# Normalising: ten constant products on TensorE beside VectorE's statistics

## What is computed

```python
def _layernorm(x, axis=-1, eps=1e-05):
    m = jnp.mean(x, axis=axis, keepdims=True)
    v = jnp.var(x, axis=axis, keepdims=True)
    return (x - m) / jnp.sqrt(v + eps)

x = x + _L0_xattn_ref(_layernorm(x, axis=-1), fside_BxSxS_0, ctx_1024, ctx_1024, ...)
x = x + _L0_attn_ref(_layernorm(x, axis=-1), L0_attn_q_w, ...)
x = x + _L0_ffn_ref(_layernorm(x, axis=-1), L0_ffn_w1s, ...)
x = x + _L1_xattn_ref(_layernorm(x, axis=-1), ctx_1024, ctx_1024, ...)
...
x = x + _L3_ffn_ref(_layernorm(x, axis=-1), L3_ffn_Wq, ...)
```

## Time and profile before

| | |
|---|---|
| median of 3 runs | 2808.99 us (2806.58 to 2811.42) |
| profiled execution | 2812.88 us, span 2811.0 us |
| TensorE busy in the span | 2357.8 us (84%) |
| VectorE busy | 1502.4 us (53%) |
| ScalarE busy | 1047.6 us (37%) |
| GpSimd busy | 300.6 us (11%) |
| mean granted TensorE clock | 0.88 |

### The profile page before, as it was taken

The page is one execution under the profiler, slowest core; times in us unless marked ns, Lnnn a source line. Parts: engine busy times, 40 slices in busy tenths (PEclk is TensorE's granted clock), DMA queues, the critical chain, the costliest instruction groups (busy, mean ns, idle before and its releaser), DMA issues. The chain is left out here.

```text
span 2811.0 us, 38689 instructions
## 1 busy us (share of the span) xinstructions
PE 2357.8 (84%) x15016; PEld 1377.6 (49%) x15016; DVE 1502.4 (53%) x2414; ACT 1047.6 (37%) x1874; POOL 300.6 (11%) x595
## 2 busy tenths in 40 slices
PE   2999999778998798999995866866879799698778
PEld 1344444335797463444443542432227657365447
DVE  4778777332221457888863862337986433223433
ACT  2566666412110234777772641213212233021310
POOL 2453000000000300000001510100000000000100
PEclk8899999987999897999997677876778899888889
DMA  6977443010453897555420001001004440200200
GB/s 188 244 184 168 92 91 61 26 69 1 180 225 129 258 279 187 95 121 98 92 30 33 12 1 58 28 1 61 0 0 150 154 161 1 92 3 0 99 0 8
DMA packets 108214, 258.60 MB, mean 92 GB/s; under 512 B 11808, under 2 KB 83072, under 8 KB 94080
## 3 DMA queue, kind: packets, MB, share of 16 engines
q1 hardware_dynamic: 101696, 203.71, 27.5%
q0 software_dynamic: 2736, 39.37, 4.1%
q10 hardware_dynamic: 3600, 13.04, 1.2%
HBM read 211.26 MB, written 44.83 MB: 91 GB/s over the span
## 5 line engine op out<-in xcount | busy, mean ns | idle before, releaser
L666 DVE TENSOR_REDUCE sta_parts<-sta_psA 128x1 f32<-128x1024 f32 x544 | 625.8, 1187 | 188.3 <-PE sta_psA L583 186.6
L724 ACT ACTIVATE sta_probs<-sta_psS 128x512 f32<-128x512 f32 x1056 | 575.9, 597 | 274.8 <-PE sta_psS L594 272.8
L594 PE MATMUL sta_psS<-L_xattn_qS,L_xattn_kst 99*128 99x256 bf16 x2112 | 356.3, 278 | 11.4 <-ACT sta_probs L724 6.6
L583 PE MATMUL sta_psA<-L_xattn_kst,L_xattn_qS 99*128 99x512 bf16 x1088 | 293.3, 387 | 46.9 <-PEq L59 32.1
L594 PEld LDWEIGHTS sta_psS<-L_xattn_qS,L_xattn_kst 99*128 99x128 bf16 x2112 | 161.4, 98 | 259.4 <-ACT sta_probs L724 183.1
L603 PE MATMUL sta_psO<-sta_probs,L_xattna_V 128*32 128x256 f32 x2560 | 189.5, 385 | 0.0
L583 PEld LDWEIGHTS sta_psA<-L_xattn_kst,L_xattn_qS 99*128 99x128 bf16 x1088 | 104.3, 99 | 131.7 <-DVE sta_parts L666 43.8
L202 ACT ACT_TABLE_LOAD x14 | 18.0, 1283 | 339.0 <-PEq L59 339.0
L2357 PE MATMUL l2t_psY<-l2t_hc,top_consts_weights 128*128 128x512 f32 x128 | 93.5, 845 | 30.7 <-DVE l2t_hc L2393 30.6
L603 PE MATMUL sta_psO<-sta_probs,L_xattn_V 128*32 128x256 f32 x1536 | 114.8, 390 | 0.0
L1008 ACT ACTIVATE sht_probs<-sht_psS 128x768 f32<-128x768 f32 (+1 forms) x64 | 55.3, 863 | 152.8 <-PE sht_psS L852 101.3
(11 more groups left out here) (617 smaller groups left out, 3973.5 us busy)
## 6 DMA issues: line engine op xcount, KB each, us to landing
L_xattn_kst<-L_xattn_keys SPq DMA_DIRECT2D x186, 136.0 KB, 5.0
L_xattn_kst<-L_xattn_keys SPq DMA_DIRECT2D x186, 128.0 KB, 4.6
L_xattn_values<-prj_rows SPq DMA_DIRECT2D x64, 256.0 KB, 3.7
L_xattn_keys<-prj_parts SPq DMA_DIRECT2D x32, 384.0 KB, 4.0
L_xattna_V<-in_ctxV SPq DMA_DIRECT2D x5, 2048.0 KB, 11.8
L_xattna_V<-L_xattn_values SPq DMA_DIRECT2D x5, 2048.0 KB, 11.0
l2f_W<-in_M SPq DMA_DIRECT2D x10, 1024.0 KB, 7.6
L_xattn_keys<-sta_bparts SPq DMA_DIRECT2D x24, 384.0 KB, 8.2
```

What stands on the lines that cost most here:

```text
L583: last = nc.tensor.matmul(psA[:, u % 2, col:col + rhs.shape[1]], lhsT, rhs, start=True, stop=True)
L594: last = nc.tensor.matmul(psS[:, at % 2, j * T:(j + 1) * T], lhsT, rhs, start=True, stop=True)
L666: nc.vector.tensor_reduce(into(parts[:, u // n % 2]), view(psA[:, u % 2, :]), AX.X, ALU.max).then_inc(max_taken, 1)
L724: nc.scalar.activation(probs[:, u % NP, i * 512:(i + 1) * 512], psS[:, at % 2, :], ACT.Exp, scale=scale).then_inc(probs_ready, 1)
```

## The change

TensorE gets ten matrix products at the start of the stage, ahead of its wait for the first tile. Each multiplies `ident16` by `mask16` and writes one PSUM bank, `psI`, that nobody reads. No semaphore is tied to them. This happens in 13 of the 15 calls: not in that of L0_xattn, where `ident16` and `mask16` aren't there yet, and not in the last, which returns before it. Nothing is removed.

```diff
-def normalize(nc, K, X, xn, xnT, eps, rms=False, w=None):
+def normalize(nc, K, X, xn, xnT, eps, rms=False, w=None, fill=True):
...
         psT = p.ps("psT", [P, KC, 512])
+        psI = p.ps("psI", [P, 512])
...
             @block.tensor
             def _(pe):
                 if xnT is None:
                     return
+                for _ in range(10 if fill else 0):
+                    nc.tensor.matmul(psI[:], K["ident16"], K["mask16_q"], start=True, stop=True)
                 for t in range(NT):
                     pe.wait_ge(rows_ready, t + 1)
...
-                normalize(nc, K, X, xn, xnT, 1e-5)
+                normalize(nc, K, X, xn, xnT, 1e-5, fill=False)
```

## The result

| | before | after |
|---|---|---|
| median | 2808.34 us (2806.45 to 2811.42, 6 runs) | 2797.82 us (2793.30 to 2799.62, 6 runs) |
| profiled execution, span | 2812.88 us, 2811.0 us | 2799.62 us, 2797.8 us |
| mean granted clock | 0.88 | 0.892 |

The ratio is 0.9962, with a 95% interval from 0.9951 to 0.9973: 10.5 us or 0.4% faster. The spans of the two traces differ by 13.2 us, more than the medians do: the traced execution of before was 4.5 us above its median, that of the changed kernel 1.8 us.

What follows compares the result with a forecast made beforehand. TensorE, often at the low clock, was taken as the bound behind the calls. Gains of 17.5, 1.5 and 0.9 us less 3.0 and 1.0 gave 15.9 us; 2797.0 less 3.9 for the median gave 2793 us, range 2784 to 2806.

Steps and rivals of the forecast that it cites:

- What bounds the kernel: Whole kernel: TensorE is busy 84% of the time, and behind the calls it is the bound at the low clock.
- The cost of the ten products: At the stage's start: ten cost 4.3 us at the low clock, 2.2 us at the high; room 2.98 us.
- The delays in the low calls: Six plain calls whose stage starts at low clock: later transposes lose 0.5 us each, 3.0 us in all.
- the five high calls: Calls whose stage starts at high clock: faster transposes gain 0.3 us in each of five, 1.5 us in all.
- The products behind: Behind eight plain calls: high clock halves 34.95 us of products, 17.5 us gained, 1.0 us taken off for misses.
- one third of a stretch: L0_attn, behind a wait of 3.08 us: one third of half of 5.66 us counted, 0.9 us gained.
- the sum: Whole kernel: 17.5 + 1.5 + 0.9 - 3.0 - 1.0 = 15.9 us gained, forecast 2793 us.
- rival D: Whole kernel: fill dropped or too late, or gains given back in later stages; time stays 2809 us; chance 0.05.
- A: At the fills: the clock takes no notice of this work, which only delays, 10 us; 2819 us; chance 0.1.
- B: Between fill and products: clock rises but falls again, half of eight stretches missed, 7.7 us gained, 2801 us; chance 0.15.
- C: Clock also holds in L0_attn and two root-mean-square calls, delays small: 24 us gained, 2785 us; chance 0.1.

## Why the prediction was right, and where it wasn't

**What bounds the kernel: right.** Behind the calls TensorE was the bound, and its clock alone was missing: with the same number of products but one row, which leaves the clock low, nothing is won and 14 us are lost.

**The cost of the ten products: right.** They ran at 0.43 us apiece at the low clock and 0.22 at the high one. Where the stage starts high nothing was delayed.

**The delays in the low calls: half as large.** Forecast 3.0 us. The transposes end 4.93 (L0_attn), 5.27 (L1_xattn), 6.06 (L1_attn), 5.49 (L2_xattn), 4.82 (L3_xattn) and 4.62 us (L3_attn) after the start; against 4.95 that is 1.5 us in sum. The extra 0.6 to 0.8 us in three of these calls with fourteen products didn't show in the total. In the five high calls for which 1.5 us of gain were forecast the transposes end 2.3 us sooner in sum.

**The products behind: right near the calls.** With delays and transposes 15.9 us were forecast, and 15.5 are there at the ends of the stretches of this trace. L2_ffn missed its stretch, L1_attn had nearly the full delay; L2_xattn and L3_ffn came as worked out. L0_attn, for which one third of a stretch was counted, has none of it here and far more in other traces.

**The step that failed is the sum.** It added up the stretches and let each gain reach the end of the program. It gave 10 us to the calls that start high and 6.6 us to the low ones. Measured apart, the high ones bring 0.0006 of the time, 1.7 us, with at most 6.7 us; that error is clear. The low ones bring 11.5 us (6.5 to 16.6), which is more by its middle, though 6.6 us is just inside. If the middles hold, the two errors have opposite signs, and it is in part luck that the total of 10.5 us came out inside the range. Of the 5.4 us between the forecast gain and the measured one, 0.4 are missing at the stretches' ends and 2.3 in the sections; the other 2.7 are the difference between the pair of traces and the medians. The prediction named the mechanism as its rival D, "given back in later stages", but only for all of the gain and with 0.05. It belonged into the sum, as a share of every term.

**The rivals.** A falls: the clock rises on zeros too, when all rows are at work. Had the clock taken no notice, its price of 10 us would have been too low, as the one-row kernel shows. B, a clock that falls before the products, occurred in L2_ffn and L0_attn of the changed kernel's trace; it isn't what took most of the missing time. Its 2801 us is 3 us from the median, nearer than the forecast of 2793, but not for its reason. C's clock that holds in L0_attn came in three traces without anything done for it.

**What stays open.** The lengths of sections over all the traces repeat a part of the pattern. With a fill of full rows in the call, L1_xattn takes 580.6 to 583.3 us (eight traces) and 584.3 to 585.2 without one (five), L2_xattn 135.0 to 139.6 against 138.1 to 142.4; by their middles both win more than was forecast. L0_ffn, among kernels with one row in the clearing of psY, takes 238.5 to 238.9 against 239.3 to 239.9: about half is kept. L3_ffn keeps 0.3 of 2.6 us. L2_attn takes some 247 us in five of its seven traces with a fill, longer than the 245.6 of the kernel before, but also in three of six without one. Why the low calls raise what they win while the high ones lose it isn't shown beyond the two places seen (L0_ffn's rise, L3_ffn's fall) and a section that answers to a shift of 0.93 us with 2.8. And since the unchanged kernel differs by 3.8 us in one section from one trace to the next, the share of luck in the 11.5 us isn't known.

## What to carry to other kernels

Where TensorE waits while another engine works and then bounds the next stage at the low clock, fill the wait with products that use all 128 rows (fewer columns weren't tried); zeros will do. Between seven and fourteen products no difference could be told in the total, though seven left the clock low in two calls. Look for work that keeps TensorE busy without raising its clock, such as clearing a bank with one row, and try it with all its rows: the clock rose sooner, but that it shortens the whole isn't shown. A few us won before a long, uneven stretch may not be there at its end: measure such calls apart, over several executions, and don't add up windows of one trace.

## What the runs showed of the hardware

- With ten products of one row of 128 and the transposes behind them TensorE was busy for 6.17 of 6.20 us, and the clock stayed at 0.50 (ratio 1.0050); 128 rows of zeros raised it (0.9958) just as data did (0.9962).
- The same wait of 3.08 us in L0_attn, behind the same ten products, left the clock high in one trace (four products in 1.95 us behind it) and low in another (3.75 us).
- The section of L3_ffn became 2.8 us longer for a delay of 0.93 us and 3.4 us longer for one of 1.85 us, and no shorter for 2.6 us won inside it.
- One section of an unchanged kernel took 149.09 us in one trace and 145.31 in the next.
